# Readerless TensorE products put in front of four steps of the expert chains

## The chip, the cores and the metric

The program runs on one core of one Trainium2 chip. The time is device time in microseconds (us) of one execution. The kernel before takes 982.8 us, the median of three runs (980.64, 982.80 and 985.89 us). The execution that the profiler recorded took 983.22 us; its first and last instruction lie 981.6 us apart.

## The reference, cut to what matters

Two batches of 1024 tokens, 128 channels, float32. Four sublayers follow each other, each added to its input and normalised over the channels:

```python
x = _layernorm(x + retention(x, ...))          # 8 heads, decay, gate
x = _layernorm(x + _L0_ffn_ref(x, ...))        # causal latent attention, then experts
x = _layernorm(x + _L1_attn_ref(x, ...))       # 16 heads of width 8, two masked corners
x = _layernorm(x + ternary_linear(x, ...))

# inside _L0_ffn_ref
x = x + mla_attention(rmsnorm(x, norm1_w), ...)
x = x + moe(rmsnorm(x, norm2_w), ...)
logits = x @ gate_w.T + gate_b                 # 4 experts
top = jnp.argmax(logits, axis=-1)
h = relu(einsum('btd,ehd->bteh', x, W1) + b1)  # hidden width 512
y = einsum('bteh,edh->bted', h, W2) + b2       # the row of expert `top` is kept
```

Only the chosen expert is computed in the kernel: the tokens are sorted by expert into 11 tiles of 128 rows.

## The kernel before, in words

Up to about 260 us the kernel computes the retention sublayer over 16 tiles of 128 tokens, with the latent projections of batch 0 beside it. Then comes one long stage that holds both attentions, the experts and the last linear layer. It is written as one list, `order()`, that every engine walks from top to bottom, each doing its own part of every entry. So no engine overtakes the list: an instruction that waits holds everything behind it on its engine.

The backbone of the list are the attention units. A unit is 128 keys against up to 512 queries of 4 heads. Its entries are:

- A (`L1577`, with masks `L1582` and `L1587`): products for the row maxima, which VectorE (DVE) reads with one reduction (`L2031`, or `L2028` where the tile is half as wide);
- M (`L1629`): the turned maxima of a block; ScalarE copies them (`L1919`), GpSimd splits them into three bf16 parts (`L1433` to `L1436`) and stores them beside the queries (`L1443`);
- S (`L1657`, masks `L1666`): the scores, which ScalarE (ACT) turns into exponentials (`L1851`, `L1847`);
- V (`L1692`): exponentials times values, 4 heads. O, N and Y (`L1700`, `L1707`, `L1715`) turn, normalise and project a finished block.

A runs 8 to 12 units ahead of S. PSUM has eight banks: four (0 to 3) form a ring for everything but S and V, three (4 to 6) take the scores, and one takes V. An entry of the ring waits in `emptied(pe, before[r])` until the entry that last held its bank has been read.

The experts of a batch are put between the attention units of the following half stage, batch 0 from about 438 to 530 us, batch 1 from about 613 to 730 us. Their entries, in order:

- norm (GpSimd, `L1453`): the rows of the experts' norm; it raises `e_normed`.
- H, twice per batch (`L1723`): four turnings each, 128x128 in float32. They wait for `e_normed`. ACT copies them out (`L1925`).
- G, once (`L1731`): the logits, 8 products with 4 columns. DVE reads them and picks the expert (`L2060` to `L2072`), which raises `e_picked`.
- C, once (`L1739`, `L1743`): the ranks of the tokens, 9 small bf16 products, after `e_picked`. DVE reads them (`L2077`) and computes each token's slot (up to `L2088`).
- sort (GpSimd, `L1460`): 8 indirect DMAs to the slots. Then the sorted rows come back, x (`L1752`), h (`L1767`) and y (`L1775`) compute the experts, and sum, stat, root and scale (`L2141`) give the normalised rows of the next sublayer.
- D, twice per batch (`L1783`): four turnings of the scaled rows, after `x1_ready`. DVE copies them out (`L2145`); the projections q, k (`L1788`) and v (`L1793`) read the copy.

The places of all entries are written out: a step for each, and a table `MOVED` that moves some by half steps. `WARMED`, added by the change, stands beside that table.

The kernel already has products without a reader: `warm(bk, n)` (`L1529`) multiplies the identity with four mask tiles, 128x128 by 128x512 in bf16, n times into a bank whose content nobody needs. Entries "warm" call it around 247 to 275 us and from 960 us on, and the first score of block 1 has eight of them.

Of the kernel before, what the change touches and what calls it, by code (L numbers as in the profile page):

```python
# [43 lines left out]
C = 512  # L44
QT = C // P
MAXIMA = HG * QT
O_LAG, N_LAG, Y_LAG = 2, 4, 6
MOVED = {
    "D": {1: -0.5},
    "D17a": {15: 0.5},  # L50
# [173 lines left out]
def build(nc, d, out, phases=5):  # L224
    ctx = ExitStack()
    with ctx:
# [7 lines left out]
        def bank(b):  # L234
            return PS[:, b, :]
# [809 lines left out]
        S_BANK, SCORES, AV_BANK = 4, 3, 7  # L1045
# [97 lines left out]
        def order():  # L1143
# [32 lines left out]
            for s in sorted(planned):  # L1176
                for kind, k in planned[s]:
                    half_steps = int(2 * (s + MOVED.get(kind, {}).get(k, 0)))
                    step = (half_steps + 1) // 2
# [48 lines left out]
        def emptied(eng, items):  # L1228

            of_dve = [by_dve[r] for r in items if ring[r][0] not in BY_ACT]  # L1230
            of_act = [by_act[r] for r in items if ring[r][0] in BY_ACT or ring[r][0] in BY_BOTH]
            if of_dve:
                eng.wait_ge(ring_dve, max(of_dve))
            if of_act:
                eng.wait_ge(ring_act, max(of_act))
# [11 lines left out]
        def attention():  # L1247
            def ring_bank(r):
                return home[r]

            @block.sync
            def _(sp):
# [65 lines left out]
                def load_steer(b):  # L1318
                    sp.wait_ge(e_steered, b + 1)
                    _, values = nc.values_load_multi_w_load_instructions(  # L1320
                        whose_i[0:1, 0, :], (mybir.EngineType.SP,), min_val=0, max_val=(NE - 1) * HID,
                        skip_runtime_bounds_check_because="a count of at most 3 of 3 comparisons, times 512")
                    return values
# [199 lines left out]
            def _(pe):  # L1523

                pe.wait_ge(load["mask"], 16)
                def warm(bk, n):

                    for _ in range(n):
                        nc.tensor.matmul(bk, identb, masks[:, 4:8, :].rearrange("p m q -> p (m q)"), start=True, stop=True)  # L1529
# [3 lines left out]
                for kind, k in order():  # L1533
                    if kind in RINGED:
                        r = place[kind, k]
                        bk = bank(ring_bank(r))
                        emptied(pe, before[r])
                        for q in (q for q, u in opened.items() if u == r):
                            pe.wait_ge(o_kept if q >= 2 else g_silu, NTILE)
                    if kind == "D16a":  # L1540
                        pe.wait_ge(g_silu, k)
                        pe.wait_ge(y_added, k - 1)
# [87 lines left out]
                    elif kind == "S":  # L1630
# [9 lines left out]
                        use = score_use[s, x]  # L1640
                        if use + 1 >= SCORES:
                            pe.wait_ge(exp_done, exps_of[use + 1 - SCORES])
                        if x == 0 and kt == 0:
                            if m == 1:
                                warm(bank(S_BANK + use % SCORES), 8)
                            pe.wait_ge(mrow[m % 2], PARTS * 16 * (m // 2 + 1))
# [335 lines left out]
            def _(dve):  # L1982
# [19 lines left out]
                for kind, k in order():  # L2002
# [116 lines left out]
                    elif kind == "y":  # L2119

                        b, i = k
                        if i == 0:
                            dve.wait_ge(e_steered, b + 1)
                            _, steer[b] = nc.values_load_multi_w_load_instructions(
                                whose_i[0:1, 1, :], (mybir.EngineType.DVE,), min_val=0, max_val=(NE - 1) * P,
                                skip_runtime_bounds_check_because="a count of at most 3 of 3 comparisons, times 128")
# [123 lines left out]
```

## Time and profile before

| | |
|---|---|
| median of three runs | 982.8 us |
| the profiled execution's own time | 983.22 us |
| its span, first to last instruction | 981.6 us |
| TensorE (PE) busy | 876.7 us, 89% of the span |
| VectorE (DVE) busy | 763.0 us, 78% |
| ScalarE (ACT) busy | 654.7 us, 67% |
| GpSimd (POOL) busy | 354.1 us, 36% |
| granted TensorE clock, mean | 0.975 of 2.4 GHz |

"Busy" is the union of the instructions' times on one engine. PE's busy time counts a product until its result has landed, so consecutive products overlap in it, and a busy PE is not one that could take nothing more. The granted clock is 1.00 at 2.4 GHz and 0.50 at 1.2 GHz; a value between them is a mean over a stretch in which it changed. "Idle before, <-X" says how long an engine stood before an instruction and what ended that.

### The profile page before, as it was taken

What the parts mean: (1) busy time and instruction counts of PE and PEld (TensorE: products, weight loads), DVE (VectorE), ACT (ScalarE), POOL (GpSimd) and SP (SyncE); (2) the same over time, 40 slices, a digit from 0 to 9 for tenths busy, and PEclk for the clock granted to TensorE, in tenths of its full rate; (3) what the DMA queues carried; (4) which work ended last, traced back from release to release, by engine and by line L of the source; (5) the groups of instructions that cost most, each with busy time, mean ns of one, the idle gap of its engine ahead of it and who ended that gap; (6) DMA issues with size and microseconds to landing.
All of it is one profiled execution on the core that took longest, in us unless ns stands there. A gap on an engine that the chain in (4) does not pass through costs nothing.

```text
span 981.6 us, 22916 instructions
## 1 busy us (share of the span) xinstructions
PE 876.7 (89%) x9121; PEld 443.7 (45%) x9127; DVE 763.0 (78%) x1156; ACT 654.7 (67%) x1285; POOL 354.1 (36%) x575
## 2 busy tenths in 40 slices
PE   7999899999878989986889689979989999999985
PEld 5777777778522444443563222326322222222232
DVE  5676676866587778887568599866889999999855
ACT  2556556666336867875556568655778888999972
POOL 1543667567342642235255112432451112111340
PEclk9999999999899999999998999989999999999999
DMA  8000000200501143121420620033106000100000
GB/s 307 1 2 2 1 2 1 76 1 2 155 4 40 35 146 120 37 59 53 120 73 2 189 59 24 12 104 94 53 2 208 21 21 21 38 4 2 5 23 22
DMA packets 49597, 52.52 MB, mean 54 GB/s; under 512 B 9066, under 2 KB 40810, under 8 KB 49332
## 3 DMA queue, kind: packets, MB, share of 16 engines
q1 hardware_dynamic: 45204, 48.12, 16.3%
q0 software_dynamic: 4288, 2.94, 1.1%
q8 instruction: 73, 1.20, 0.5%
q14 instruction: 32, 0.26, 0.1%
HBM read 32.37 MB, written 19.68 MB: 53 GB/s over the span
## 4 chain that ended last, share of the span: by engine, by line
PE 35%; DVE 12%; ACT 5%; issue 3%; DMA 1%; POOL 1%; another core or an unknown queue 1%; DVEq 0%; ACTq 0%; SPq 0%; POOLq 0%
PE banks L1692 12%; PE banks L1657 8%; DVE arena L2031 8%; PE banks L1577 5%; ACT arena L1851 3%; PE banks L1767 2%; PE banks L1775 2%; PE banks L1700 1%; PE banks L1788 1%; PE banks L1715 1%; DMA arena<-arena 1%; ACT arena L1864 1%; DVE arena L2028 0%; PE banks L1811 0%
## 5 line engine op out<-in xcount | busy, mean ns | idle before, releaser
L2031 DVE TENSOR_REDUCE arena<-banks 128x2 f32<-128x1024 f32 (+1 forms) x384 | 441.3, 1197 | 58.0 <-PE banks L1577 28.9
L1851 ACT ACTIVATE arena<-banks 128x512 f32<-128x512 f32 (+1 forms) x768 | 409.8, 588 | 95.4 <-PE banks L1657 64.0
L1692 PE MATMUL banks<-arena 128*9 128x256 f32 (+1 forms) x3328 | 251.2, 381 | 6.7 <-ACT arena L1864 3.9
L1657 PE MATMUL banks<-arena 61*128 61x512 bf16 (+4 forms) x896 | 165.7, 370 | 32.6 <-ACT arena L1851 17.1
L1577 PE MATMUL banks<-arena 56*128 56x512 bf16 (+3 forms) x896 | 163.2, 367 | 20.5 <-DVE arena L2031 15.0
L1657 PEld LDWEIGHTS banks<-arena 61*128 61x128 bf16 (+1 forms) x896 | 44.0, 93 | 192.7 <-ACT arena L1851 157.6
L1433 POOL CAST arena<-arena 16x128 bf16<-16x128 f32 x32 | 9.0, 281 | 293.2 <-ACT arena L1919 283.7
L1692 PEld LDWEIGHTS banks<-arena 128*9 128x9 f32 x3328 | 52.9, 89 | 134.0 <-issue 83.2
L1577 PEld LDWEIGHTS banks<-arena 56*128 56x128 bf16 x896 | 45.2, 95 | 43.4 <-DVE arena L2031 33.3
L414 POOL TENSOR_TENSOR arena<-arena 128x8 f32<-128x8 f32 (+1 forms) x35 | 50.3, 1439 | 30.0 <-DVE arena L2195 27.6
L1443 POOL DMA_DIRECT2D arena<-arena x96 | 55.2, 579 | 10.8 <-POOL arena L1436 9.3
L569 ACT ACTIVATE arena<-banks 128x1024 f32<-128x1024 f32 x16 | 16.4, 1025 | 58.4 <-PE banks L519 51.8
L594 DVE TENSOR_TENSOR arena<-banks,arena 128x128 f32<-128x128 f32 x16 | 4.7, 291 | 53.9 <-PE banks L535 53.9
L561 ACT ACTIVATE arena<-banks,arena 128x128 f32<-128x128 f32 x128 | 46.2, 467 | 0.0
L1473 POOL DMA_INDIRECT expert_rows<-arena x22 | 21.4, 972 | 53.6 <-DVE arena L2127 53.0
L2028 DVE TENSOR_REDUCE arena<-banks 128x4 f32<-128x1024 f32 (+1 forms) x32 | 30.6, 958 | 12.7 <-PE banks L1587 10.1
L1847 ACT ACTIVATE arena<-banks 128x512 f32<-128x512 f32 (+1 forms) x64 | 27.9, 490 | 15.0 <-PE banks L1666 14.6
L799 PE MATMUL banks<-arena 128*128 128x128 f32 x256 | 31.9, 277 | 1.8 <-DVE arena L851 1.8
L519 PE MATMUL banks<-arena 128*128 128x128 f32 x256 | 32.6, 280 | 0.6 <-DVE arena L594 0.5
L799 PEld LDWEIGHTS banks<-arena 128*128 128x128 f32 x256 | 30.0, 191 | 5.1 <-DVE arena L851 2.8
L535 PE MATMUL banks<-arena 128*128 128x128 f32 x256 | 31.5, 275 | 0.3 <-DVE arena L582 0.3
L694 PE MATMUL banks<-arena 128*128 128x512 f32 x64 | 30.3, 594 | 1.1 <-DMA arena<-r_wqk 1.1
(241 smaller groups left out, 1398.0 us busy)
## 6 DMA issues: line engine op xcount, KB each, us to landing
arena<-k_products SPq DMA_DIRECT2D x32, 224.0 KB
arena<-q_products SPq DMA_DIRECT2D x64, 112.0 KB
arena<-e_w SPq DMA_DIRECT2D x22, 256.0 KB
q_products<-arena SPq DMA_DIRECT2D x12, 384.0 KB, 3.3
k_products<-arena SPq DMA_DIRECT2D x12, 384.0 KB, 3.9
arena<-arena POOLq DMA_DIRECT2D x96, 4.0 KB, 1.8
sorted_rows<-c_pads SPq DMA_DIRECT2D x2, 709.5 KB, 8.5
q_products<-arena SPq DMA_DIRECT2D x4, 288.0 KB, 3.9
```

Source lines behind the costliest of these rows:

```text
L414: link(eng.tensor_tensor(y, v, epst[:, 1:2].to_broadcast(list(v.shape)), ALU.pow))
L519: ins = nc.tensor.matmul(bank(s // 4)[:, (s % 4) * P:(s % 4 + 1) * P], wg[:, s * P:(s + 1) * P], XT[:, i, :], start=True, stop=True)
L535: ins = nc.tensor.matmul(bank(y_bank(i))[:, 0:P], uu[:, s, :], wo[:, s, :], start=(s == 0), stop=(s == RH - 1))
L561: ins = nc.scalar.activation(ga[:, s, :], bank(4 + s // 4)[:, (s % 4) * P:(s % 4 + 1) * P], ACT.Identity, scale=gn[:, 0, s:s + 1], bias=gn ...
L799: ins = nc.tensor.matmul(bank(2 + s // 4)[:, (s % 4) * P:(s % 4 + 1) * P], sm[:, s, :], vv[n % 2][:, s, :], start=first, stop=True, skip_g ...
L1443: g_.dma_start(rows, nmp[k % 2][:, i, :]).then_inc(mrow[k % 2], 16)
L1577: ins = nc.tensor.matmul(bank(first + par)[:, at:at + hi - lo], Qs[k_][rows, qc, y, qo:qo + P], Ks[k_][rows, y, lo:hi], start=True, stop=n ...
L1657: ins = nc.tensor.matmul(bank(S_BANK + (use + par) % SCORES)[:, at:at + C - o], Ks[n % NS][rows, y, kt * P:(kt + 1) * P], Qs[n % NS][rows, ...
L1692: ins = nc.tensor.matmul(PS[h * VROWS:h * VROWS + VW, AV_BANK, o:end], V[:, b, kt, HG * g + h, :], Pr[u % PROBS][:, h, o:end], start=(kt = ...
L1851: s_.activation(Pr[s % PROBS][:, 2 * x + par, o:C], scores[:, o:C], ACT.Exp) \
L2028: v_.tensor_reduce(of, two_banks.rearrange("p r (y e) -> p r y e", y=2)[:, :, :, 0:width], AX.X, ALU.max).then_inc(ring_dve, 1)
L2031: v_.tensor_reduce(of[:, :, x], two_banks[:, :, 0:width], AX.X, ALU.max).then_inc(ring_dve, 1)
```

## The change

A table names four kinds of entry and a number of products for each. Right after the waits for the ring bank, and ahead of the entry's own wait for its input, PE issues that many readerless products into the entry's own bank; the entry's first product then overwrites them. A second call, in front of the scores, looks up the kind "S", which the table does not hold, so it issues nothing.

```diff
 O_LAG, N_LAG, Y_LAG = 2, 4, 6
+WARMED = {"H": 4, "G": 2, "C": 8, "D": 3}
 MOVED = {
...
                         emptied(pe, before[r])
                         for q in (q for q, u in opened.items() if u == r):
                             pe.wait_ge(o_kept if q >= 2 else g_silu, NTILE)
+                        warm(bk, WARMED.get(kind, 0))
                     if kind == "D16a":
...
                         use = score_use[s, x]
                         if use + 1 >= SCORES:
                             pe.wait_ge(exp_done, exps_of[use + 1 - SCORES])
+                        warm(bank(S_BANK + use % SCORES), WARMED.get(kind, 0))
                         if x == 0 and kt == 0:
```

`warm` itself is unchanged:

```python
def warm(bk, n):

    for _ in range(n):
        nc.tensor.matmul(bk, identb, masks[:, 4:8, :].rearrange("p m q -> p (m q)"), start=True, stop=True)
```

Over the program these are 4 H x 4, 2 G x 2, 2 C x 8 and 4 D x 3, together 48 products of 128x512 and 48 weight loads. Waits, DMAs and the other engines' instructions stay as they are.

## Rows read from the trace of the kernel before

**Rows 1.** The page: share of the chain that ended last, by engine.
```profile
PE 35%; DVE 12%; ACT 5%; issue 3%; DMA 1%; POOL 1%; another core or an unknown queue 1%; DVEq 0%; ACTq 0%; SPq 0%; POOLq 0%
```

**Rows 2.** Groups of PE's instructions, shapes apart: busy us, mean ns | idle before.
```profile
L1723 PE MATMUL banks<-arena 128*128 128x128 f32 x16 | 2.2, 278 | 1.4 <-POOL arena L1453 1.4
L1783 PE MATMUL banks<-arena 128*128 128x128 f32 x16 | 2.5, 280 | 0.0
```

**Rows 3.** Timeline, start and us: the readerless products that are there already.
```profile
263.25 3.60 PE L1529 MATMUL banks<-arena 128*128 128x512 bf16 x8
...
962.62 0.81 PE L1529 MATMUL banks<-arena 128*128 128x512 bf16 x3
...
964.69 4.48 PE L1529 MATMUL banks<-arena 128*128 128x512 bf16 x20
```

**Rows 4.** Timeline around both H of batch 0.
```profile
437.76 2.04 DVE L2028 TENSOR_REDUCE arena<-banks 128x4 f32<-128x1024 f32 x2 [0.38 <-PE banks L1587]
...
438.45 1.90 POOL L1453 TENSOR_TENSOR arena<-arena 128x1024 f32<-128x1024 f32 x1
...
440.50 1.06 PE L1723 MATMUL banks<-arena 128*128 128x128 f32 x8 [1.44 <-POOL arena L1453]
```

**Rows 5.** Timeline around G and C of batch 0.
```profile
445.71 0.19 DVE L2060 TENSOR_TENSOR arena<-banks,arena 128x32 f32<-128x32 f32 x1 [0.74 <-PE banks L1731]
...
450.11 0.34 PE L1743 MATMUL banks<-arena 128*128 128x32 bf16 x8
...
450.70 0.18 DVE L2077 TENSOR_TENSOR arena<-banks,arena 128x32 f32<-128x32 f32 x1
```

**Rows 6.** Timeline around H, G and C of batch 1.
```profile
616.34 1.09 PE L1723 MATMUL banks<-arena 128*128 128x128 f32 x8
...
617.03 1.27 ACT L1925 ACTIVATE arena<-banks,arena 128x512 f32<-128x512 f32 x2 [0.27 <-PE banks L1723]
...
621.93 0.19 DVE L2060 TENSOR_TENSOR arena<-banks,arena 128x32 f32<-128x32 f32 x1 [1.21 <-PE banks L1731]
...
625.81 3.49 DVE L2031 TENSOR_REDUCE arena<-banks 128x2 f32<-128x1024 f32 x3
...
628.44 0.34 PE L1743 MATMUL banks<-arena 128*128 128x32 bf16 x8
```

**Rows 7.** Chain that ended last, pieces at the four D: start, us, what.
```profile
524.89 0.59 PE banks L1783 x4
...
528.56 0.56 PE banks L1783 x4
...
718.46 1.23 DVE arena L2031
719.68 0.60 DVE arena L2145
...
723.82 0.44 PE banks L1783 x4
```

**Rows 8.** Timeline: the third D itself.
```profile
718.94 0.60 PE L1783 MATMUL banks<-arena 128*128 128x128 f32 x4
```

**Rows 9.** Mean granted TensorE clock of the execution.
```profile
core 0: 981.6 us, clock 0.975
```

**Rows 10.** Stretches at the lower clock: length, busy time by engine, then PEclk.
```profile
461.50:468.50 7.00, 3.35 (x24) 0.52 (x24) 2.79 (x3) 2.89 (x6) 6.06 (x11) 0.51 0.53 143
516.00:523.50 7.50, 6.32 (x41) 1.61 (x41) 6.81 (x12) 2.92 (x6) 5.83 (x13) 0.54 0.01 1
622.00:625.30 3.30, 3.30 (x20) 1.02 (x16) 2.97 (x14) 1.09 (x2) 1.92 (x4) 0.50 0.05 9
642.80:649.30 6.50, 5.61 (x38) 0.92 (x38) 4.23 (x4) 4.24 (x8) 0.59 (x1) 0.50 0.43 114
```

**Rows 11.** Chain, the same O turning at the lower and the full clock.
```profile
623.70 1.05 PE banks L1700 x4
...
651.79 0.59 PE banks L1700 x4
```

**Rows 12.** Chain, waits in the two stretches in which the tokens are sorted.
```profile
460.73 3.72 another core or an unknown queue
...
636.53 3.50 issue
```

## The prediction

> **What bounds the kernel now.** I read the chain that ended last first. Its shares say that no engine alone sets the time, but that PE is by far the most frequent member, with DVE second [rows 1]. All engines walk one list in order, so a PE instruction put into the list costs its full time wherever PE is the chain's member or feeds it, and nothing where PE stands waiting anyway. The second view is therefore the idle time in front of the four kinds of entry that get products. By group, H shows 1.4 us of idle time over all its 16 records and D shows 0.0 [rows 2]. The reader is to see there that, of twelve places, one has a wait that could hide something. The third view is the timeline around each place, to see who reads the result and whether that reader was already late. The fourth is the granted clock by stretches, since that is the one thing that a readerless product can give back.
>
> **The price of one product.** The kernel has such products at its end: 20 of them take 4.48 us and 3 take 0.81 us at the full clock, so one costs (4.48 - 0.81) / 17 = 0.216 us [rows 3]. At the lower clock 8 take 3.60 us, 0.45 us each at most [rows 3]. Its weight load lies beside the product before. 48 products cost 48 x 0.216 = 10.4 us of PE time at the full clock; that is the upper bound, and the sum below takes away what is covered.
>
> **H, batch 0 (2 x 4 products).** Before the first H, PE stands idle for 1.44 us, from 439.06 to 440.50, until POOL's norm ends at 440.35 [rows 4]. Its bank was last read by the first of the two reductions that start at 437.76 and take 2.04 together, so it is free at about 438.8 [rows 4], and 4 x 0.216 = 0.86 us of products fit in: 0. If that norm came 1 us earlier, they would cost up to 0.86. The second H follows with no wait between, and its four products stand in front of it: 0.86. ACT and G wait for that H.
>
> **G, batch 0 (2).** DVE stands idle for 0.74 us until the logits land [rows 5], so DVE is late by every PE delay: 0.43.
>
> **C, batch 0 (8).** 8 x 0.216 = 1.73 us. The ranks have landed at 450.11 + 0.34 = 450.45 and DVE reads them at 450.70, when it has finished its reductions [rows 5]. So 0.25 us is covered and 1.48 is added. The rank chain on DVE leads to the sort, and A's next bank is released by the same read. Batch 0 without D: 0.86 + 0.43 + 1.48 = 2.77.
>
> **H, G, C, batch 1.** Here neither H has idle time, and ACT stands waiting for the first (0.27 us) [rows 6]: 8 x 0.216 = 1.73. DVE waits 1.21 us for G [rows 6]: 0.43. The ranks land at 628.78, while DVE is busy with three reductions until 629.30 [rows 6]; I take 0.43 us as covered, because the read begins just before the modelled end, and 1.30 of C's 1.73 is added. Together 3.46.
>
> **D (4 x 3 products, 0.65 us each).** Three of the four D are pieces of the chain themselves (524.89, 528.56 and 723.82) [rows 7]: 3 x 0.65. At the third D the chain is on DVE, whose reduction ends at 719.69 [rows 7]; the turnings land at 718.94 + 0.60 = 719.54 [rows 8], so 0.15 is covered and 0.50 is added. Together 2.45. What is queued behind D on PE is the next scores and the q and k projections, and ACT, POOL and the storing of the next sublayer's parts wait for those.
>
> The products come to 2.77 + 3.46 + 2.45 = 8.7 us. The bounds are 10.4 us (nothing covered) and, if each of the delays is absorbed in a later wait, 0.
>
> The second call, in front of S, finds no number: 0 products, and the name is looked up when the program is built.
>
> **What the clock gives back.** The mean granted clock is 0.975 [rows 9], so some 5% of the span, about 49 us, ran at the lower level. One of these stretches lies directly behind a place of the change: 622.0 to 625.3, at 0.50, right after G of batch 1, with PE busy through all of it and no idle time before it [rows 10]. An O turning takes 1.05 us in it against 0.59 at the full clock [rows 11]. With 2 large products in front of G and 8 in front of the H before it, I expect that this fall does not come: 3.30 / 2 = 1.65 us back, rounded down to 1.5, as not all of PE's time there scales. Its bounds are 0 (the fall comes all the same, or at another entry) and 1.65. The fall is no property of G: behind G of batch 0, whose work is the same, there was none.
>
> Sum: 8.7 - 1.5 = 7.2 us. The profiled execution took 983.22 us, of which 981.6 are the span and 1.6 lie around it; it stands 0.4 us above the median of 982.8. From the execution 990.4, from the median 990.0. I forecast 990.0 us.
>
> **Rivals.**
>
> *The clock is worth more than the products (not slower).* Place: the four stretches of the expert chains at the lower clock. If readerless products kept the clock full through them, half of PE's busy time in each would come back: 3.35 / 2 + 6.32 / 2 + 3.30 / 2 + 5.61 / 2 = 9.3 us [rows 10], against 8.7 paid: 982.2 us, no change. It decides at the stretch from 516.0: only where that one and one of the two sort stretches shorten does the gain reach the cost, and below 978 us also the waits would have to take in most of the products. For it speaks the size of these stretches. Against it speaks where they begin: at 461.5 and 642.8 PE had been standing in the sort's stalls [rows 12], 11 and 14 us behind C, and the one from 516.0 is over (523.5) before the first D begins (524.89) [rows 7, 10]. No product stands in front of those three.
> The Trainium skill, TensorE: Matmul & The Clock Gate, section "A second HAM failure mode: psum-queue depth-cycling", says that frequent short idle times between groups of matmuls make the clock swing between its two levels, and that throughput is lost to the way back up. By that rule, filling such gaps is right and this rival would be the forecast. The trace agrees only in part: three of the four stretches in rows 10 begin at waits without any product in front, and eleven of the twelve places of the change have no gap to fill.
>
> *The sort's stalls swallow the delays.* Behind both C the chain has a wait of 3.72 and one of 3.50 us with no instruction of an engine as its cause [rows 12]. If their ends are fixed by something that doesn't move with PE, the 2.77 and 3.46 us in front of them vanish, and 2.45 of D less 1.5 of the clock remain: 983.8 us. For it: these waits are longer than the delays. Against it: the sort is issued after the slots, and the slots after C, so a late C makes a late sort.
>
> *Nothing comes back.* The fall behind G comes anyway, and products that meet a lower clock cost up to 0.45 instead of 0.216: 982.8 + 8.7, up to 982.8 + 10.4, so 991.5 to 993.2 us. For it: the lower clock at 516.0 to 523.5 came without any product near. Against it: a fuller PE has no reason to fall more often.
>
> **How the numbers follow.** The forecast has 0.50 (from 986 to 991.5), the clock rival 0.22, the swallowed delays 0.18, and nothing back 0.10. A measurement of this kernel can tell about 0.5%, 4.9 us, from no change: below 977.9 is faster, above 987.7 slower. Slower: 0.42 of the forecast's 0.50 and all 0.10 of the last rival, 0.52. Faster: 0.12, the tail of the clock rival. The rest, 0.36, is within. The range must reach over the two rivals on the lower side and take in the full cost above: 979.5 to 993.5 us. The forecast's own range is 986 to 991.5.
>
> **What would show it.** In the changed kernel's timeline, 48 more records of the product line, in groups of 4, 2, 8 and 3, some 0.216 us apart. DVE's wait for the logits grows by what stands in front of them (0.74 and 1.21 us), and before the read of the ranks a new wait of about 1.5 us stands, released by C. The third view is the position of the same entry in both traces: the first S behind C of batch 0 is late by 2.8 us, the x entry of batch 1 by some 6 less 1.5, and the last D by 7. If the stalls of 3.7 and 3.5 us shrink by as much as the entries ahead of them are late, the second rival is right. If the mean granted clock rises from 0.975 to 0.985 or more, the first is; 0.5 x 1.5 / 981.6 of it (0.001 to 0.002) belongs to my forecast. The prediction is wrong if the time is below 987, and its mechanism is wrong if the entries behind C are not late.

## The result, and the profile after

The changed kernel takes 990.7 us (four executions, 988.9 to 994.1) against 981.7 us of the kernel before on the same chip (four, 979.4 to 985.9): 1.0091 times as long, 95% interval 1.0069 to 1.0114, so 8.9 us slower. The forecast was 990.0 us. The execution that the profiler recorded took 989.66 us, with a span of 988.0.

The page of the changed kernel gives the same picture as before: the chain's shares answer to [rows 1] and the clock to [rows 9]. Its second line here names the engines, the third and fourth are groups with busy us, mean ns and the idle time before them.

```profile
core 0: 988.0 us, clock 0.976
PE 34%; DVE 13%; ACT 5%; issue 3%; POOL 1%; DMA 1%; another core or an unknown queue 1%; DVEq 0%; ACTq 0%; SPq 0%; POOLq 0%
L1726 PE MATMUL banks<-arena 128*128 128x128 f32 x16 | 2.5, 276 | 0.3 <-POOL arena L1454 0.3
L1786 PE MATMUL banks<-arena 128*128 128x128 f32 x16 | 2.4, 272 | 0.0
```

The idle time before H has fallen from 1.4 to 0.3 us [rows 2]. The rest of these lines is within one per cent of the span, or 0.3 us, of before. The cost isn't seen in shares. It is seen at the places themselves. First the timeline around H and G of batch 0, which answers to [rows 4, 5]: start, us, engine, line, and in brackets the idle time before and its releaser.

```profile
437.77 0.66 PE L1726 MATMUL banks<-arena 128*128 128x128 f32 x4 [0.32 <-POOL arena L1454]
438.27 1.03 PE L1530 MATMUL banks<-arena 128*128 128x512 bf16 x4
...
444.18 0.19 DVE L2063 TENSOR_TENSOR arena<-banks,arena 128x32 f32<-128x32 f32 x1 [1.09 <-PE banks L1734]
```

The first H still waits for POOL, 0.32 us instead of 1.44, so its four products lie inside the old wait. The second H follows its products. (DVE's instructions have moved from L2060 to L2063 and from L2077 to L2080, as the change adds lines above them.) DVE's wait for the logits is 1.09 us instead of 0.74. The same for C of batch 0 [rows 5]:

```profile
448.66 1.67 PE L1530 MATMUL banks<-arena 128*128 128x512 bf16 x7 [0.16 <-issue]
...
450.20 0.34 PE L1746 MATMUL banks<-arena 128*128 128x32 bf16 x8
...
450.58 0.19 DVE L2080 TENSOR_TENSOR arena<-banks,arena 128x32 f32<-128x32 f32 x1 [1.42 <-PE banks L1746]
```

Here is the new wait of about 1.5 us in front of the read of the ranks, released by C. (Of eight products the trace holds seven records.) And batch 1 [rows 6], where ACT's wait for the first H has grown from 0.27 to 1.09 us and DVE's for G from 1.21 to 1.64:

```profile
616.27 0.81 PE L1530 MATMUL banks<-arena 128*128 128x512 bf16 x3 [0.16 <-issue]
...
617.56 0.69 ACT L1928 ACTIVATE arena<-banks,arena 128x512 f32<-128x512 f32 x1 [1.09 <-PE banks L1726]
...
623.60 0.19 DVE L2063 TENSOR_TENSOR arena<-banks,arena 128x32 f32<-128x32 f32 x1 [1.64 <-PE banks L1734]
...
632.15 0.19 DVE L2080 TENSOR_TENSOR arena<-banks,arena 128x32 f32<-128x32 f32 x1 [1.25 <-PE banks L1746]
```

In the chain that ended last the products are now pieces of their own: in batch 0 at the second H, G, C and both D, in batch 1 at every entry of the change. Three of these places (start, us, what). These answer to [rows 7]:

```profile
438.43 0.86 PE banks L1530 x4
439.29 0.44 PE banks L1726 x4
...
448.66 1.67 PE banks L1530 x7
...
721.65 0.59 PE banks L1530 x2
722.24 0.45 PE banks L1786 x4
```

The stretches at the lower clock from C of batch 0 on, with the columns of [rows 10]: length, busy us by engine, clock, share of DMA, GB/s. (Another, from 558.7 to 565.5, lies outside the expert chains and is left out.) The fourth row isn't at the lower clock; it is the stretch around H and G of batch 1.

```profile
456.30:459.70 3.40, 3.40 (x24) 0.50 (x24) 3.00 (x9) 2.05 (x4) 2.48 (x4) 0.50 0.17 58
463.10:469.90 6.80, 4.89 (x32) 0.70 (x36) 3.68 (x3) 3.63 (x7) 5.04 (x9) 0.50 0.69 177
514.30:517.70 3.40, 3.13 (x24) 0.65 (x22) 3.33 (x18) 2.25 (x5) 0.96 (x2) 0.50 0.00 0
615.00:630.00 15.00, 13.32 (x122) 5.90 (x123) 10.50 (x23) 8.96 (x18) 3.11 (x7) 1.00 0.01 3
644.00:650.80 6.80, 5.70 (x42) 0.93 (x38) 4.72 (x4) 3.85 (x7) 2.29 (x2) 0.50 0.44 118
760.10:763.50 3.40, 3.23 (x20) 0.55 (x24) 1.44 (x2) 1.73 (x4) 0.00 (x0) 0.50 0.59 139
```

The fall behind G of batch 1 did not come, as forecast. Two others are new: one at 456.3, 6 us behind C of batch 0 with its eight products, and one at 760.1, in a stretch that the forecast did not look at.

### The third view: how late the same entry is

Both programs give DVE the same instructions in the same order, so each one's start can be set against its start in the trace of before. The table gives this lateness in us at some of them, for every kernel that was profiled. A column is a place, and what counts is the step from one column to the next. "H+", "G", "C" are the DVE instruction before the first H, the read of the logits and the read of the ranks; "sort" is one behind the wait of the sort; "D-" and "D" stand before and behind a pair of D.

```
            batch 0                                 batch 1
            H+     G      C      sort   D-     D    H+     G      C      sort   D-     D      740us  760us
base         0.37   0.37   0.36  -4.92  -6.40  -6.40  -5.63  -5.63  -5.71 -11.08 -11.21 -11.21 -11.21 -10.97
base_b       3.74   3.72   3.71  -1.57  -3.38  -3.37  -5.04  -5.04  -5.11 -10.49 -10.35  -9.41  -9.41  -9.30
after       -2.63  -1.54  -0.13   0.57   0.31   1.21  -0.30   1.67   2.94   2.61   2.49   3.58   3.56   6.65
again       -2.96  -1.86  -0.46  -5.74  -8.42  -7.51 -10.31  -8.34  -7.08 -12.45 -12.58 -11.49 -11.49  -8.81
quiet        0.22   1.31   3.69  -1.59  -3.25  -2.22  -3.54  -1.50   1.80  -3.57  -2.45  -0.61  -0.62  -0.82
c_32         1.10   1.10   7.79   2.52   0.43   0.42   0.47   0.47   6.91   1.55   1.41   1.41   1.40   1.21
twice        1.18   3.88   7.12   1.85   0.09   2.29   1.33   5.46   8.45   3.08   4.41   6.79   6.79   6.60
only_h      -1.75  -0.95  -0.38   0.31   0.31   0.30  -1.13   0.41   0.33  -0.35  -0.45  -0.44  -0.45   0.28
only_g      -2.01  -1.67  -1.77  -7.05  -9.47  -8.43  -9.26  -8.83  -8.91 -14.28 -14.42 -13.86 -13.87 -13.71
only_c      -2.05  -2.06  -0.56   0.06  -0.12  -0.13  -1.81  -1.82  -0.56  -1.18  -1.25  -1.25  -1.25  -1.44
only_d      -3.37  -3.37  -3.37  -2.93  -2.83  -1.54  -3.01  -3.02  -3.09  -3.08  -2.52  -0.10  -0.10  -0.16
covered     -2.40  -2.47  -1.91  -1.21  -2.08  -2.09  -3.44  -3.44  -3.47  -3.47  -3.13  -3.13  -3.13  -3.32
rows_first  -1.47  -0.38   1.03   0.17  -1.43  -0.52  -2.85  -0.88   0.38   0.30   0.69   1.78   1.77   1.59
```

Two things have to be known to read it. The first column starts anywhere between -3.4 and +3.7 us, although no product of the change has touched DVE's work by then; base and base_b, one kernel on one chip, are 3.4 us apart there. So a position by itself says little. (The last two columns are DVE instructions at 745.1 and 761.6 us of before.) And there are two kinds of chips: on some (those of again, quiet, c_32, twice, only_g, base and base_b) the kernel before takes 970 us, on the others 981 to 982. In the table the faster ones show as a drop of 5.3 us from C to sort in both batches.

For after the steps are: H and G of batch 0 +1.09, C +1.41, the first two D +0.90, H and G of batch 1 +1.97, C +1.27, the last two D +1.09. Together 7.7 us. The same steps in again are 1.10, 1.40, 0.91, 1.97, 1.26 and 1.09, also 7.7. Against its own start (-2.63), after is 2.5 us late behind C of batch 0, 5.2 behind the sort of batch 1 and 6.2 behind the last D, where the forecast had 2.8, 4.5 and 7.

### The profile page after: what moved, and what is told of

It reads as the page before. It is cut to its first block, busy times and chain, and to the rows that moved or that the text cites. A ratio compares the mean times of both kernels' runs of the same rounds, so it can differ in the third digit from the quotient of the medians.

```text
span 988.0 us, 22993 instructions
## 1 busy us (share of the span) xinstructions
PE 885.3 (90%) x9162; PEld 447.9 (45%) x9175; DVE 764.5 (77%) x1156; ACT 655.0 (66%) x1285; POOL 350.5 (35%) x575
## 4 chain that ended last, share of the span: by engine, by line
PE 34%; DVE 13%; ACT 5%; issue 3%; POOL 1%; DMA 1%; another core or an unknown queue 1%; DVEq 0%; ACTq 0%; SPq 0%; POOLq 0%
PE banks L1695 11%; DVE arena L2034 9%; PE banks L1660 8%; PE banks L1579 5%; ACT arena L1854 3%; PE banks L1770 2%; PE banks L1778 2%; PE banks L1530 1%; PE banks L1703 1%; PE banks L1791 1%; DMA arena<-arena 1%; PE banks L1718 1%; ACT arena L1867 1%; PE banks L1814 0%
## 5 line engine op out<-in xcount | busy, mean ns | idle before, releaser
L1660 PE MATMUL banks<-arena 61*128 61x512 bf16 (+4 forms) x896 | 165.4, 369 | 35.0 <-ACT arena L1854 16.2
L1660 PEld LDWEIGHTS banks<-arena 61*128 61x128 bf16 (+1 forms) x896 | 43.9, 93 | 195.4 <-ACT arena L1854 153.4
L1444 POOL DMA_DIRECT2D arena<-arena x96 | 55.1, 577 | 10.8 <-POOL arena L1437 9.3
L2031 DVE TENSOR_REDUCE arena<-banks 128x4 f32<-128x1024 f32 (+1 forms) x32 | 30.6, 957 | 12.3 <-PE banks L1589 9.6
L1530 PE MATMUL banks<-arena 128*128 128x512 bf16 x112 | 31.1, 399 | 1.8 <-issue 1.2
```

The lines of the kernel that those rows point to most:

```text
L1444: g_.dma_start(rows, nmp[k % 2][:, i, :]).then_inc(mrow[k % 2], 16)
L1660: ins = nc.tensor.matmul(bank(S_BANK + (use + par) % SCORES)[:, at:at + C - o], Ks[n % NS][rows, y, kt * P:(kt + 1) * P], Qs[n % NS][rows, ...
```

## The experiments

The kernels that keep part of the change differ in one line, the numbers of products by kind of entry. Products in front of nothing are 0.

```diff
-WARMED = {"H": 4, "G": 2, "C": 8, "D": 3}
+WARMED = {"C": 32}                             # c_32
+WARMED = {"H": 8, "G": 4, "C": 16, "D": 6}     # twice
+WARMED = {"C": 8}                              # only_c; only_h {"H": 4}, only_g {"G": 2}, only_d {"D": 3}
```

### The whole change again, more of it, and products that are not large

**again** is the changed kernel with nothing altered, on the chip of the next three.

> The changed kernel once more, on the chip on which the next three run, so that they can be set against it. By the theory that every product without cover costs its 0.216 us on the chain, it is 7 to 10 us slower than before, as at first (8.9 us between the medians).

Measured: 977.8 us against 970.4 (eleven executions of before), ratio 1.0083 (1.0058 to 1.0107), which is 8.1 us, or 7.4 between the medians. The cost is much the same on a chip on which both kernels are 11 to 13 us faster.

**c_32** puts 32 products in front of each C and none elsewhere.

> Only in front of the two C (the ranks), 32 large products each, 6.9 us per batch. Full cost theory: 2 x 6.9 less the 0.25 and 0.43 us of cover, 13.1 us over before, whether it comes before the sort's stall or not. If the stalls of 3.7 and 3.5 us behind C swallow what PE is late by, 5.9 us over before. If the clock pays back half of the stretches behind C (1.7 and 2.8 us), 8.6 us.

Measured: 982.8 us, 1.0121 (1.0102 to 1.0140), which is 12.3 us. The timeline at C of batch 0:

```profile
451.39 6.85 PE L1530 MATMUL banks<-arena 128*128 128x512 bf16 x31 [0.16 <-issue]
458.11 0.34 PE L1746 MATMUL banks<-arena 128*128 128x32 bf16 x8
458.49 0.19 DVE L2080 TENSOR_TENSOR arena<-banks,arena 128x32 f32<-128x32 f32 x1 [6.61 <-PE banks L1746]
```

32 x 0.216 = 6.91 us, of which DVE feels 6.61 as a wait. The table has +6.69 and +6.44 us from G to C. The drop from C to sort is 5.27 and 5.36 us, as in base (5.28 and 5.37), although c_32 is 7.4 us later than base at the one C and 12.6 at the other. So also a delay of this size is passed on through the sort whole: of 13.1 us put on the chain 12.3 came out. What this run can't do is decide the two rivals that it was meant for. On this kind of chip the engines don't stand still behind C (see the last section), and base has no stretch at the lower clock there, so there was neither a wait to swallow the delay nor a lower clock to win back. That test is only_c, below.

**twice** doubles every number.

> All four numbers doubled (H 8, G 4, C 16, D 6), 96 products. Full cost: the first H of batch 0 has 1.4 us of idle time for 1.7 us of products, so 0.3; the second H 1.7, G 0.9, C 3.2; batch 1 3.5 + 0.9 + 3.0; D 5.0: 18.5 us over before, or 17 with 1.5 back from the clock, about twice the first result. If the loss comes from one place or from the mere shift of the code and not from the number of products, it is near the 9 us of the changed kernel.

Measured: 988.2 us, 1.0190 (1.0170 to 1.0210), 17.8 us. Its steps in the table are 2.70, 3.24, 2.20, 4.13, 2.99 and 2.38 us, 17.6 together. The first set of products costs 7.7 us, the second 9.9 of the 10.4 that its 48 products take, as the covered parts are used up by the first. So the cost goes with the number of products and not with the mere shift of the code.

**quiet** keeps the places and numbers but takes products of the same length that are only 4 columns wide.

```diff
+                def quiet(bk, n):
+                    for _ in range(n):
+                        nc.tensor.matmul(bk[:, 0:NE], ident, ident[:, 0:NE], start=True, stop=True)
-                        warm(bk, WARMED.get(kind, 0))
+                        quiet(bk, WARMED.get(kind, 0))
```

> The same 48 places, but each large product (128x512, bf16, 0.216 us) is replaced by one small float32 product of 128x4, the kind of the logits, which the trace of before shows at 1.92 us for 8 of them, 0.23 us each. PE is taken for the same time (48 x 0.23 = 11.0 us against 10.4) with hardly any columns. If all that counts is PE's time, it is as slow as the changed kernel, plus 0.5 us. If the large products pay a part back by the clock (1.5 us was forecast, 9.3 by the clock rival), it is slower than the changed kernel by that much and its mean granted clock is lower by 0.001 to 0.002, or by 0.009.

Measured: 984.2 us, 1.0149 (1.0128 to 1.0169): 13.8 us, 6.4 more than again on the same chip. The mean granted clock over all timed executions is 0.975 for quiet and 0.985 for again; (1 - clock) x span is 24.6 and 14.8 us. Stretches at the lower clock stand beside the places in quiet, where again has none (columns as above):

```profile
447.50:450.90 3.40, 3.40 (x42) 1.18 (x40) 3.12 (x10) 1.65 (x4) 1.77 (x3) 0.50 0.03 4
621.60:628.40 6.80, 6.02 (x36) 1.26 (x39) 4.99 (x11) 3.04 (x7) 0.67 (x2) 0.50 0.02 2
717.20:720.60 3.40, 3.40 (x23) 1.16 (x23) 2.47 (x7) 1.08 (x2) 2.88 (x7) 0.50 0.01 1
```

PE is busy through two of these and nearly through the third. So what stands on PE matters to the clock, and not only that it is busy. But quiet shows what small products lose, not what large ones gain over none: against before, again has 0.985 and before 0.982 on that chip. Some of the 6.4 us lies at the places themselves: their steps add up to 11.7 us in quiet and 7.7 in again, most of it at C (2.38 and 3.30 us against 1.40 and 1.26). The result lies between the 1.5 and the 9.3 us that were expected of the clock, so it confirms neither size.

### One kind of entry at a time

These ran on a chip on which before takes 981.8 us (35 executions), with 12 executions each.

> Only the 4 products in front of each H. Full cost with the first H of batch 0 covered by its wait: 0.86 + 1.73 = 2.6 us over before. Without that cover 3.5. If products ahead of G keep the clock full behind it, up to 1.65 us less.

> Only the 3 products in front of each D. Full cost: 2.45 us over before, of which the first two D bring 1.3 and the last two 1.15. If the wait for the next stack's load, 25 us behind the first two D, takes them in, 1.15.

> Only the 8 products in front of each C. Full cost less cover: 1.48 + 1.30 = 2.8 us over before. If the sort's stalls swallow the delay: 0.

Measured: only_h 984.1 us, 1.0021 (1.0004 to 1.0038); only_d 983.3, 1.0019 (1.0000 to 1.0038); only_c 983.5, 1.0014 (0.9999 to 1.0029). By the table, only_h steps by 0.80 and 1.54 us, only_c by 1.50 and 1.26, only_d by 1.29 in batch 0 and 2.42 around the third and fourth D. That last number is twice what after has there (1.09), and a fall of the clock stands at the third D, with PE busy for most of it and DVE waiting 1.87 us for the turnings (columns as above):

```profile
715.20:718.60 3.40, 3.16 (x15) 1.30 (x17) 1.65 (x3) 0.27 (x1) 0.97 (x3) 0.50 0.00 0
```

Here, then, a fall goes with some 1.3 us more (one trace): that matters for the clock term below. Of what the terms of the sum say for each kind (2.6, 2.8 and 2.5 us), 1.4 to 2.1 us arrive in the time; the intervals hold both.

In only_c the instructions that wait through the sort show what the second rival was about (timeline, ACT and DVE):

```profile
463.96 1.08 ACT L1854 ACTIVATE arena<-banks 128x512 f32<-128x512 f32 x2 [3.78 <-remote]
463.97 1.23 DVE L2034 TENSOR_REDUCE arena<-banks 128x2 f32<-128x1024 f32 x1 [3.12 <-remote]
```

The wait is there in full although C was 1.5 us later (before has 3.77 us on ACT and 3.11 on DVE, after 4.49 and 3.15), and the lateness behind it is +0.06, from -0.56 at C and -2.06 before it. Behind the second C the lateness falls by 0.62 us; only_h, with no product at C, has +0.69 and -0.68 at the same two steps, so that is not a delay swallowed. On this kind of chip, where the standstill exists, a delay goes through: the rival of the swallowed delays falls here.

**only_g** tests the clock term: G was the entry behind which the fall stood.

> Only the 2 products in front of each G (the logits). Full cost: 0.43 us each, 0.9 us over before. In the traces so far the clock fell within 8 us behind a G in 6 of 14 cases without large products at G, and in 0 of 6 with them; if that is their doing, half of 3.4 us comes back in 0.43 of the cases at two places, 1.5 us, and the kernel is 0.6 us faster than before. Either is near what 5 rounds can tell; the falls behind the two G in the trace tell more.

Measured: 972.1 us against 970.1, 1.0023 (1.0006 to 1.0041). The table shows the two products as +0.34 and +0.43 us. Nothing came back; but base and base_b, on this same chip, have no fall behind G either, so there was none to take away. Over all traces a fall begins within 2 us of the read of the logits at 6 of the 18 G without large products in front and at none of the 10 with them. That the products keep it away is thus likely and not shown.

### Is a fall behind G worth anything?

**base** and **base_b** are the kernel before, unchanged, one profile each.

> The kernel before, unchanged, for a second trace of it. Positions of the same entries show how much of the 2.6 us by which the changed kernel was ahead at the first H, and of the 3 us that it lost at 755 us, is there between two executions of one program: the theory that the products alone make the difference expects that two executions of this kernel differ by 1 to 3 us at those places too.

> The same once more: a third trace, for the same question. By the theory of cost the entries behind C are no later in any of the three against H of the same trace, while they are 1.4 us later in the changed kernel.

Measured: 972.4 and 973.6 us. In base the stretch around G of batch 1 is at the full clock:

```profile
610.00:622.00 12.00, 10.33 (x105) 4.62 (x101) 9.47 (x22) 7.83 (x16) 3.10 (x7) 1.00 0.02 3
```

In the trace of before, the same stretch has the fall from 622.0 to 625.3 [rows 10]. Without it, base should be earlier at C than at H by up to 1.65 us. It is earlier by 0.08 us (-5.63 to -5.71), base_b by 0.07. And covered, the kernel of the next experiment, has neither products nor anything else changed there and shows the same fall as before, with PE busy throughout:

```profile
618.50:621.90 3.40, 3.40 (x20) 1.05 (x16) 3.07 (x14) 1.08 (x2) 1.97 (x4) 0.50 0.05 9
```

Its step from H+ to C is -0.03 us. With the fall 0.00 and -0.03, without it -0.08 and -0.07: the fall is worth 0.1 us at most. DVE's reductions set the pace there, and PE at half speed was still in time. At the third D, where DVE waits for PE, a fall as long went with 1.3 us more in only_d. base was also to show whether the 3 us at 740 to 760 us come and go in one program: base and base_b step by 0.24 and 0.11 us there, so they don't.

### Products where they are covered

**covered** takes all products away and puts 4 in front of the first H of batch 0 and 8 in front of the first row-maxima products of block 16, where PE waits for a stack.

```diff
-WARMED = {"H": 4, "G": 2, "C": 8, "D": 3}
+WARMED = {}
-                        warm(bk, WARMED.get(kind, 0))
+                        if (kind, k) == ("H", (0, 0)):
+                            warm(bk, 4)
...
+                            if m == BLOCKS:
+                                warm(bk, 8)
```

> Products only where PE waits anyway: 4 in front of the first H of batch 0 (1.44 us of idle time there before) and 8 in front of the first maxima product of the second attention, where PE waits 2.26 us for the load of the queries and the granted clock fell right after it. The cost theory says 0 for the products; what the clock gives back is at most half of a stretch of 3.4 us, so between 0 and 1.7 us faster than before. If a readerless product costs something even in a wait, it is slower.

Measured: 984.0 us, 1.0018 (0.9998 to 1.0039). The timeline at H and at block 16:

```profile
436.87 0.81 PE L1530 MATMUL banks<-arena 128*128 128x512 bf16 x3 [0.21 <-issue]
438.00 1.09 PE L1729 MATMUL banks<-arena 128*128 128x128 f32 x8 [0.32 <-POOL arena L1454]
...
549.38 1.67 PE L1530 MATMUL banks<-arena 128*128 128x512 bf16 x7 [0.16 <-issue]
550.99 0.61 PE L1582 MATMUL banks<-arena 56*128 56x512 bf16 x4
```

H waits for POOL with or without its four, and the step over H and G is -0.07 us: the cover in the first term of the sum is right. But the products bought nothing either, and no version that was run beats the kernel before.

### The step from 740 to 760 us

After and again lose 3.1 and 2.7 us between 740 and 760 us, where the change puts nothing. The timeline of after shows what the first scores of block 22 waited for (POOL stores three max rows, SyncE's queue loads the next stacks, PE is L1660):

```profile
753.68 1.68 POOL L1444 DMA_DIRECT2D arena<-arena  x3 [0.29 <-POOL arena L1437]
754.50 0.79 SPq L1295 DMA_DIRECT2D arena<-k_products  x2
755.33 1.74 SPq L1297 DMA_DIRECT2D arena<-q_products  x2
...
760.27 0.61 PE L1660 MATMUL banks<-arena 61*128 61x512 bf16 x2 [2.01 <-DMA arena<-arena]
```

And before, where PE has no such wait:

```profile
750.11 1.68 POOL L1443 DMA_DIRECT2D arena<-arena  x3 [0.29 <-POOL arena L1436]
751.41 0.78 SPq L1294 DMA_DIRECT2D arena<-k_products  x2
```

The loads are issued 1.3 us behind the first row in before, and 0.8 us in after, and there the third row takes 5.34 us to land instead of 3.46. PE waits 2.01 us (again: 1.71), and the fall at 760.1 begins at the end of that idle time.

The other traces bear this out. In again the distance is 0.85 us and the third row takes 5.03. In only_h it is 0.91, the row takes 4.20, and 0.73 us are lost. In only_c and covered it is 0.93, the row takes 3.13 and 3.25, and nothing is lost. In twice the loads come 2.3 us behind the first row, the third lands in 1.74, and the step is -0.19 us, with twice the products. So the loss goes with the distance of the two queues, and not with the number of products. What sets the distance stays open.

**rows_first** is the changed kernel with one line more: SyncE waits until the rows have landed before it issues those loads.

```diff
+                sp.wait_ge(mrow[0], PARTS * 16 * 12)
                 for n in range(3 * NG, 4 * NG):
                     load_all(n)
```

> The changed kernel with one more wait: SyncE issues the stack loads behind the stores of batch 1 (second attention) only when the max rows of block 22 have landed. In both traces of the changed kernel the first scores of that block waited 2.0 and 1.7 us for these rows, whose stores were issued within 0.3 us of the first load, and 3.1 and 2.7 us were lost there in all, against 0.1 to 0.2 us in the kernel before. If the collision of the two is the cause, the wait of PE goes and the kernel is 2.5 to 3 us nearer to before than the changed one: 5 to 6 us over before instead of 7.4 to 8.9. If the loss there is only the clock, or the products' own cost, nothing changes.

Measured: 985.8 us against 981.4, 1.0056 (1.0037 to 1.0075), where the changed kernel has 1.0091 and 1.0083. Its timeline at the place:

```profile
751.88 1.68 POOL L1445 DMA_DIRECT2D arena<-arena  x3 [0.29 <-POOL arena L1438]
...
755.31 0.39 PE L1661 MATMUL banks<-arena 61*128 61x512 bf16 x2
...
756.25 0.78 SPq L1295 DMA_DIRECT2D arena<-k_products  x2
...
757.53 0.39 PE L1661 MATMUL banks<-arena 61*128 61x512 bf16 x2
```

The loads now come 4.4 us behind the first row, PE's wait is gone, and the step from 740 to 760 is -0.18 us. The two ratios of the changed kernel and this one come from different chips, and their intervals overlap a little; the gain of about 3 us rests on the step in the table, with which they agree.

## Why the prediction was right, and where it was not

**The price and the places: right.** The forecast took H and G of batch 0 at 1.29 us, C at 1.48, two D at 1.30, H and G of batch 1 at 2.16, C at 1.30, two D at 1.15: 8.7. Measured are 1.09, 1.41, 0.90, 1.97, 1.27 and 1.09: 7.7. Each is below its forecast, by 0.07 us (C of batch 0) up to 0.40 (the first two D). The cover of the first H was seen, and confirmed by covered. The two C, where the reader's own lateness had to be taken off, are within 0.07 us.

**The delays pass the sort: right.** only_c shows it on a chip with the standstill behind C, which did not shrink (3.78 us on ACT, 3.77 in before). c_32 shows it for a large delay on a chip without the standstill: its entries are 7.4 us later than base at the first C and 7.4 behind its sort, 12.6 and 12.6 at the second.

**What the clock gives back: wrong in size, and by its reasoning.** This is the term of 1.5 us. The fall behind G of batch 1 did stay away, as the prediction said, though base and base_b lack it without any product. But the prediction took half of PE's busy time in it as gained. base and base_b, which lack that fall too, gained 0.1 us by it. What the prediction left out is the question whether PE set the pace of DVE there; [rows 6] had the answer, since DVE runs three reductions without a gap from 625.81 and the ranks wait for it, and in the fall itself DVE was busy for 2.97 of 3.30 us [rows 10].

**Not foreseen: a collision of DMAs.** 3.1 us in the profile of after at 740 to 760 us. It comes from the timing of two DMA queues against each other and not from PE's work: rows_first and twice don't have it. The prediction followed the last D's delay to its readers and no further, so it never asked what DMAs lie close together 20 us behind it.

**The sum.** 7.7 of products and 3.1 of the collision are 10.8; the ratio's interval says 8.9 us, give or take 2.2. Neither is far from the other, but some 2 us remain, and they remain three times: again has 10.4 by its steps and 8.1 by its ratio, rows_first 7.7 and 5.5. They stay open. The profiles hold at most a part of them: between the first two D and the next H, after gains 1.5 us on before, but base_b (1.7), only_h (1.4) and only_c (1.7) do as well, so there it is the trace of before that lost time. So 990.0 was met by a clock term that was 1.4 us too good, product terms 1.0 us too dear, and 3 us that it did not have. That its value is so near the measurement is partly luck; its sign and its cause are not.

**The rivals.** The clock rival (982.2 us) is out: no falls behind the sort went away (463.1 and 644.0 are there), only the one behind G did and the one from 516.0 was half as long, while a new one stands at 456.3. The mean clock is 0.976 against 0.975, and the time is 990.7. Its rule from the Trainium skill, TensorE: Matmul & The Clock Gate, section "A second HAM failure mode: psum-queue depth-cycling", says that frequent short idle times between groups of matmuls make the clock swing. The runs agree in part: a fall began at the end of the 2.01 us of idle time before 760.27, but in covered PE had stood idle for only 0.32 us in the 8 us before the fall at 618.5, and was busy through all of it. "Nothing comes back" (991.5 to 993.2) was right about the clock behind G and in reach of the interval.

## What to carry to other kernels

A readerless product costs nearly its full time wherever PE has no idle time of its own in front of the entry and the reader isn't late anyway. One look at both per place gave the cost of each step here to within 0.4 us, and of all of them to 1.0 in 8.7. A lower clock is only worth removing where PE sets the pace, so read the chain inside the stretch before half of its busy time is booked as gain. After any shift by a few microseconds, look at the places where small DMAs with a waiting reader share the queues with large loads.

## What the runs showed of the hardware

The same program takes 970 us on some chips and 981 to 982 us on others. Nearly all of the difference, 10.6 us in base, arises around one event that comes twice. Behind each C, as the last of GpSimd's indirect DMAs are issued, ACT, DVE and PE stand still on the slower chips [rows 12], and not on the faster ones: in before each of them for 3.1 to 3.8 us in batch 0 and 2.5 to 3.5 us in batch 1. In again, ACT and DVE run through it:

```profile
458.00 10.00 DVE L2034 TENSOR_REDUCE arena<-banks 128x2 f32<-128x1024 f32 x9
...
460.57 3.35 ACT L1854 ACTIVATE arena<-banks 128x512 f32<-128x512 f32 x6 [1.20 <-PE banks L1660]
```

Both together, the standstill and the stretch at the lower clock that follows it on the slower chips alone, make 5.3 us per batch. A difference between kernels is therefore only to be read against before on the same chip. And at 438 us of the span, where no product of the change has come yet, the traces lie up to 7.1 us apart, so a position means nothing without its step.
